# The end of a two-layer kernel reordered: the last eight skip terms go to TensorE, and the last norm's first four tiles are transposed together

## The reference

```
x      = silu(conv(proj))                       # 8 groups x 8 channel tiles of 128
y      = Y_diag + Y_off * decay + D * x         # D * x is the skip term
y      = y * rsqrt(mean(y*y) + eps) * norm_w * silu(gate)
h      = h + y @ out_proj.T                     # residual
n      = layernorm(h)
out    = h + n @ W_up.T + LoRA(chosen expert, n)
```

## Time and profile before

| | |
|---|---|
| median of 3 runs | 1755.25 us (1753.87 to 1755.78) |
| profiled execution, whole | 1755.16 us |
| its span in the trace | 1753.2 us |
| TensorE busy | 1686.0 us, 96% of the span |
| VectorE, ScalarE, GpSimd busy | 68%, 72%, 42% |
| mean granted TensorE clock | 0.98 |

### The profile page before, as it was taken

How to read it: one execution, slowest core, us unless ns; L and a number is a source line. 1 busy time by engine, 2 the same in 40 slices (tenths; PEclk the granted TensorE clock), 3 DMA queues, 4 the chain that set the end, 5 groups by cost and what they waited for, 6 DMA issues and landing times.

```text
span 1753.2 us, 26728 instructions
## 1 busy us (share of the span) xinstructions
PE 1686.0 (96%) x9420; PEld 1379.0 (79%) x9420; DVE 1192.9 (68%) x1868; ACT 1270.3 (72%) x2173; POOL 732.6 (42%) x794
## 2 busy tenths in 40 slices
PE   6998799999999999999999999999999999999978
PEld 5876577788888888888888888888888888888767
DVE  5665676866676767676766776677767676767773
ACT  3332138986888778877987798779877887888831
POOL 3543023444444344433444345344444444344550
PEclk9998799999999999999999999999999999999989
DMA  4310215323232323232333232323232323232401
GB/s 164 112 67 1 78 61 168 116 85 105 85 111 90 111 85 117 85 116 73 111 100 101 85 109 92 115 71 120 93 105 83 109 90 112 92 109 69 141 14 48
DMA packets 98564, 166.45 MB, mean 95 GB/s; under 512 B 11616, under 2 KB 49888, under 8 KB 96768
## 3 DMA queue, kind: packets, MB, share of 16 engines
q1 hardware_dynamic: 98432, 164.75, 28.9%
HBM read 158.43 MB, written 6.29 MB: 94 GB/s over the span
## 4 chain that ended last, share of the span: by engine, by line
PE 81%; DVE 4%; ACT 2%; issue 1%; POOL 0%; POOLq 0%; DVEq 0%; ACTq 0%
PE bank L203 22%; PE bank L205 21%; PE bank L204 21%; PE bank L1819 7%; PE bank L1829 4%; PE bank L1809 3%; PE bank L1887 1%; DVE m_xc L1556 1%; DVE m_gate L1556 0%; ACT m_mt L1318 0%; DVE m_xc L1490 0%; PE bank L1934 0%; DVE m_wo_l L1585 0%; DVE m_gate L1472 0%; PE bank L194 0%
## 5 line engine op out<-in xcount | busy, mean ns | idle before, releaser
L203 PE MATMUL bank<-xh,w_h 128*128 128x512 f32 x1152 | 463.4, 402 | 3.4 <-DVE m_xc L1556 2.9
L205 PE MATMUL bank<-xh,w_l 128*128 128x512 f32 x1152 | 451.5, 392 | 0.0
L204 PE MATMUL bank<-xl,w_h 128*128 128x512 f32 x1152 | 449.2, 390 | 0.0
L1233 POOL TENSOR_TENSOR m_z_l<-m_zg,m_z_h 128x512 fp32r<-128x512 f32 x128 | 177.4, 1386 | 572.7 <-ACT m_z_h L1394 572.7
L1318 ACT ACTIVATE m_mt<-m_mt,m_unit 128x128 f32<-128x128 f32 x1024 | 312.0, 389 | 0.0
L1212 POOL TENSOR_TENSOR w_l<-w_raw,w_h 128x512 fp32r<-128x512 f32 x144 | 187.2, 1300 | 231.1 <-ACT w_h L1285 231.1
L1567 DVE TENSOR_TENSOR x<-x,bank 128x512 f32<-128x512 f32 x128 | 87.8, 686 | 270.5 <-PE bank L205 270.2
L203 PEld LDWEIGHTS bank<-xh,w_h 128*128 128x128 f32 x1152 | 216.8, 188 | 55.6 <-issue 13.6
L205 PEld LDWEIGHTS bank<-xh,w_l 128*128 128x128 f32 x1152 | 216.5, 188 | 47.4
L1556 DVE SCALAR_TENSOR_TENSOR m_xc<-bank,m_par_conv,m_xc 128x1020 f32<-128x1020 f32 (+2 forms) x192 | 244.6, 1274 | 10.1 <-ACT m_xc L1297 5.2
L204 PEld LDWEIGHTS bank<-xl,w_h 128*128 128x128 f32 x1152 | 217.1, 188 | 41.3
(11 more groups left out here) (270 smaller groups left out, 2775.7 us busy)
## 6 DMA issues: line engine op xcount, KB each, us to landing
m_mt<-ncs_rows SPq DMA_DIRECT2D x128, 512.0 KB, 3.7
w_raw<-w_in SPq DMA_DIRECT2D x144, 256.0 KB, 3.1
m_wo_raw<-w_out_in SPq DMA_DIRECT2D x64, 256.0 KB, 5.1
m_e<-ecs_rows SPq DMA_DIRECT2D x128, 128.0 KB, 3.5
a_wo_raw<-wo_in SPq DMA_DIRECT2D x8, 1024.0 KB, 4.9
x<-x_in SPq DMA_DIRECT2D x8, 256.0 KB, 4.6
a_wq_raw<-wq_in SPq DMA_DIRECT2D x8, 256.0 KB, 4.5
x_saved<-x SPq DMA_DIRECT2D x1, 2048.0 KB, 8.5
```

Source lines behind the costliest of these rows:

```text
L203: nc.tensor.matmul(out, ah, bh, start=first, stop=False)
L204: nc.tensor.matmul(out, ah, bl, start=False, stop=False)
L205: return nc.tensor.matmul(out, al, bh, start=False, stop=last)
L1233: nc.gpsimd.tensor_tensor(z_l[:, s % 2, :, :], zg[:], f(z_h[:, s % 2, :, :]), ALU.subtract).then_inc(zl_ready, 1)
```

## The change

DVE no longer multiplies x by D in the last eight steps: four diagonal matrices are built once, and PE adds D * x into bank 4. `add_up` (in every group) issues the eight matmuls that need only z_h first and waits for z_l before the last four. Expert weight splits and the residual for tiles 0 and 1 move. The first four normalised tiles are transposed one after the other into banks 0, 1, 4, 5. The fourth `base` of each half moves behind `turn_lora`. The tiles xeh and xel lie elsewhere in memory, over first halves of two buffers that are used no more.

```diff
@@ turn_bank
-        return t % 2 if t < HT else (t + 1) % 2
+        return (0, 1, 4, 5)[t] if t < HT else (t + 1) % 2
@@ POOL, step / after run
-                if kind == "last" and NT + 2 <= s < NT + 6:
-                    (a_low if s < NT + 4 else base_low)((s - NT) % 2)
+                if kind == "last" and s in (NT + 2, NT + 3):
+                    a_low(s % 2)
                 if kind == "last" and s == STEPS - 2:
-                    for t in range(3):
-                        add_residual(t)
+                    add_residual(2)
+                    add_residual(3)
...
             run(step, prepare)
-            add_residual(3)
-            base_low(2)
-            base_low(3)
+            pool.wait_ge(xn_ready, HT)
+            for k in range(KT):
+                base_low(k)
@@ ACT, step
-                if kind == "last" and s in (NT + 2, NT + 3):
-                    ks = slice(2 * (s % 2), 2 * (s % 2) + 2)
-                    nc.scalar.activation(wb_h[:, ks, :], wb_raw[:, ks, :], ACT.Copy).then_inc(ew_hi, 1)
-                if kind == "last" and s == NT + 4:
-                    nc.scalar.activation(b_h, b_raw, ACT.Copy).then_inc(ew_hi, 1)
                 if kind == "last" and s == STEPS - 2:
                     act.wait_ge(crs_ready, 1)
-                    for t in range(HT):
+                    for t in (2, 3):
                         nc.scalar.activation(acc[:, t, :], ...).then_inc(scaled, 1)
+                    for ks in (slice(0, 2), slice(2, 4)):
+                        nc.scalar.activation(wb_h[:, ks, :], wb_raw[:, ks, :], ACT.Copy).then_inc(ew_hi, 1)
+                    nc.scalar.activation(b_h, b_raw, ACT.Copy).then_inc(ew_hi, 1)
@@ ACT, high / after run
             def high(t):
+                act.wait_ge(y_ready, at(LAST, STEPS - 1))
...
             high(0)
+            high(1)
+            high(2)
+            high(3)
             root_of_sums(1)
-            high(1)
             read_a(0)
-            high(2)
             read_a(1)
-            high(3)
@@ DVE, step
+                if s == NT - 1 and kind == "last":
+                    dve.wait_ge(w_split, tile_at(LAST, LEAD - 1))
+                    for ct in range(CT):
+                        nc.vector.tensor_scalar(d_mat[:, ct, :], ident[:], par_dn[:, CT + ct:CT + ct + 1], None,
+                                                ALU.mult).then_inc(d_ready, 1)
...
+                    whole = bank[:, 4, :].rearrange("p (c l) -> p c l", c=CT)
+                    by_tensor = kind == "last" and half == 1
+                    if by_tensor and s % 2 == 0:
+                        last = nc.vector.tensor_copy(y[:], whole)
-                    for ct in range(CT):
+                    for ct in range(0 if by_tensor else CT):
...
+                    if by_tensor and s % 2 == 1:
+                        dve.wait_ge(off_ready, pair(g, s))
+                        last = nc.vector.tensor_tensor(y[:], whole, off, ALU.add)
...
-                if kind == "last" and s == STEPS - 3:
+                if kind == "last" and s == STEPS - 2:
                     sums_to_scale(0)
+                    combine(0)
@@ DVE, low
-                dve.wait_ge(ew_lo, min(t + 1, 7))
@@ DVE, after run
+            add_out(LAST, STEPS - 2)
+            combine(1)
             statistics(0)
             statistics(1)
-            add_out(LAST, STEPS - 2)
             statistics(2)
...
             low(0)
+            low(1)
             variance_of_sums(1)
-            low(1)
+            low(2)
+            low(3)
             sums_to_scale(1)
             combine(4)
             combine(5)
-            low(2)
             combine(6)
-            low(3)
             combine(7)
@@ PE, diag
-                                            start=True, stop=True)
+                                            start=h < 2 or not (g == LAST and s >= NT),
+                                            stop=not (g == LAST and s >= NT))
+                if g == LAST and s >= NT:
+                    half, t = divmod(s, NT)
+                    pe.wait_ge(d_ready, CT)
+                    for ct in range(CT):
+                        last = nc.tensor.matmul(bank[:, 4, ct * P:(ct + 1) * P], d_mat[:, ct, :],
+                                                xc[:, half, ct, t * P:(t + 1) * P], start=False, stop=ct == CT - 1)
@@ PE, add_up
-                pe.wait_ge(zl_ready, at(g, s))
+                pe.wait_ge(zh_ready, at(g, s))
                 pe.wait_ge(acc_added, at(g, s - 1))
...
                 for ct in range(CT):
-                    last = three_pass(...)
+                    if t == 0:
+                        pe.wait_ge(wo_split, wo_at(g, half, ct))
+                    nc.tensor.matmul(bank[:, 7, :], z_h[:, s % 2, ct, :], wo_h[:, ct, :], start=ct == 0, stop=False)
+                    nc.tensor.matmul(bank[:, 7, :], z_h[:, s % 2, ct, :], wo_l[:, ct, :], start=False, stop=False)
+                pe.wait_ge(zl_ready, at(g, s))
+                for ct in range(CT):
+                    last = nc.tensor.matmul(bank[:, 7, :], z_l[:, s % 2, ct, :], wo_h[:, ct, :], start=False,
+                                            stop=ct == CT - 1)
@@ PE, after run
             sums(1)
-            turn_norm(0)
-            turn_norm(1)
-            products(0)
-            turn_norm(2)
-            products(1)
-            turn_norm(3)
-            products(2)
-            products(3)
             for t in range(HT):
-                base(t)
+                turn_norm(t)
+            for t in range(HT):
+                products(t)
+            base(0)
+            base(1)
+            base(2)
             turn_lora(0)
             turn_norm(4)
+            base(3)
...
-            for t in range(HT, NT):
-                base(t)
+            base(4)
+            base(5)
+            base(6)
             turn_lora(1)
+            base(7)
```

More of the change, by code:

```diff
@@ L836, in ssm_block @@
         gate = earlier.enter_context(nc.sbuf_tensor("m_gate", [P, 2, CT, TOKENS], F32))
+    sb("first_xc", [P, CT, TOKENS])
     xeh = sb("xeh", [P, NT, KT, P], F32R)
-    sb("second_xc", [P, CT, TOKENS])
+    sb("first_gate", [P, CT, TOKENS])
     xel = sb("xel", [P, NT, KT, P], F32R)
-    sb("second_gate", [P, CT, TOKENS])
     b_cm, c_cm = gate[:, 0, 2, :], gate[:, 0, 3, :]
@@ L877, in ssm_block @@
     csmall = small_part(6 * NT).rearrange("p (i t) -> p i t", i=6)
+    d_mat = small_part(CT * P).rearrange("p (c l) -> p c l", c=CT)
     dt_loaded = sem("dt_loaded")
@@ L960, in ssm_block @@
     combined = sem("combined")
+    residual_added = sem("residual_added")
     nvar_ready = sem("nvar_ready")
@@ L975, in ssm_block @@
     stored = sem("stored")
+    d_ready = sem("d_ready")
     TILES = PROJ_TILES
@@ L1269, in add_residual @@
                 pool.wait_ge(xs_loaded[0], 16)
-                pool.wait_ge(scaled, t + 1)
-                nc.gpsimd.tensor_tensor(acc[:, t, :], acc[:, t, :], xs[:, t, :], ALU.add).then_inc(combined, 1)
+                pool.wait_ge(scaled, t - 1)
+                nc.gpsimd.tensor_tensor(acc[:, t, :], acc[:, t, :], xs[:, t, :], ALU.add).then_inc(residual_added, 1)
             run(step, prepare)
-            add_residual(3)
-            base_low(2)
-            base_low(3)
+            pool.wait_ge(xn_ready, HT)
+            for k in range(KT):
+                base_low(k)
             pool.wait_ge(ew_hi, 4)
@@ L1644, in step @@
                             in1=bank[:, 4, ct * P:(ct + 1) * P], op0=ALU.mult, op1=ALU.add)
-                    if s % 2 == 1:
+                    if by_tensor and s % 2 == 1:
+                        dve.wait_ge(off_ready, pair(g, s))
+                        last = nc.vector.tensor_tensor(y[:], whole, off, ALU.add)
+                    elif s % 2 == 1:
                         last.then_inc(dx_added, 1)
@@ L1683, in statistics @@
             def statistics(t):
-                dve.wait_ge(combined, t + 1)
+                if t in (2, 3):
+                    dve.wait_ge(residual_added, t - 1)
+                else:
+                    dve.wait_ge(combined, t + 1 if t < 2 else t - 1)
                 return n.statistics(nc, t)
@@ L1714, in combine @@
             def combine(t):
-                dve.wait_ge(xs_loaded[1], 16)
+                dve.wait_ge(xs_loaded[t // HT], 16)
                 dve.wait_ge(acc_added, at(LAST, NT + t))
@@ L1833, in add_up @@
             def add_up(g, s):
-                pe.wait_ge(zl_ready, at(g, s))
+                pe.wait_ge(zh_ready, at(g, s))
                 pe.wait_ge(acc_added, at(g, s - 1))
                 half, t = divmod(s, NT)
-                if t == 0:
-                    pe.wait_ge(wo_split, wo_at(g, half, CT - 1))
                 for ct in range(CT):
-                    last = three_pass(nc, bank[:, 7, :], z_h[:, s % 2, ct, :], z_l[:, s % 2, ct, :],
-                                      wo_h[:, ct, :], wo_l[:, ct, :], ct == 0, ct == CT - 1)
+                    if t == 0:
```

(13 more changed lines are left out.)

## The result

The changed kernel takes 1740.26 us (median of four runs, 1737.69 to 1743.35) against 1755.5 for the kernel before: 0.9914 of its time (95% interval 0.9902 to 0.9926), 15.2 us less where 12.1 were forecast. Run again with the experiments it took 1738.63 (1737.87 to 1739.35), 0.9908 (0.9894 to 0.9921), 15.45 less than its neighbours. The profiled execution took 1737.69, with a span of 1735.9.

A forecast was written before the change was run, and what follows sets the result against it. The last eight steps were taken as bound by a chain round the engines, PE nearest to full. Savings of 9.4 + 0.2 + 2.5 = 12.1 us from 1755.16 gave 1743.1, range 1739 to 1748.

The forecast's parts named there:

- inner forecast: Whole kernel: a time of 1741 to 1745.5 us, given a chance of 0.40.
- Part 1: Last eight steps, D(8) to end of U(14): PE's waits go, PE bounds at full clock, 5.1 us less.
- Part 2: Last product U(15) and norm, up to the first transpose: 4.3 us less.
- part 3: First transpose to first base: 0.2 us less, two of four products at half clock.
- The price of the skip products: Steps 8 to 15: four added PE products cost 0.92 us per step, 7.4 in all.
- Rival C: Steps 8 to 15: the chain's waits stay and the products come on top, 1755.6 to 1762.9 us; chance 0.05.
- rival B: Last group: POOL contending with DVE, ACT's step 14 or y late, +1 to +3 us, 1745; chance 0.13.
- the old 5.1 us: Norm, last statistics to first transpose: 5.1 us before, some 1.5 from drawn-out small instructions; 2.9 forecast.
- The other way of rival A: Behind the norm and in the second half's products: no half clock, -2.3 and -1.3 us, 1739.5; chance 0.13.
- rival A: Clock behind the norm: all four products at half clock, one more base caught, +2.4 to +4 us; chance 0.22.
- Part 4: Both halves, turn_lora to lora: a base covers the waits for the LoRA operands, 2.5 us less.
- Rival D: Last eight steps: PE's waits only change names, half of the first saving lost, 1747 to 1749 us; chance 0.07.

The follow-up runs named there:

- splits early: Changed kernel with the expert weight splits back in steps 10 to 13 and POOL's last two behind the steps: 1744.02 us, 0.9936 of the kernel before.
- own banks: Changed kernel with the last group's U taking turns over banks 7, 0 and 6, and scale, combines, statistics, last add_outs and turn_norm(4) moved: 1735.76 us, ratio 0.9891.
- bases first: Changed kernel with the fourth base ahead of turn_lora in both halves: 1743.66 us, 0.9937 of the kernel before.
- old add_up: Changed kernel with add_up as before in every group, three passes per weight tile behind z_l and all four weight splits: 1741.61 us, ratio 0.9928.
- interleaved order: Changed kernel with the first four tiles' transposes between the products, in banks 0 and 1, and low and high as before: 1743.71 us, ratio 0.9935.

## Why the prediction was right, and where it was not

**Direction and size**: right. 1740.26 lies in the range of 1739 to 1748, 2.8 us below the number, for the reason given: PE's waits went and PE became the bound at full clock. It lies outside the inner forecast of 1741 to 1745.5, and that the sum is no further off is in part luck: parts 1 and 2 brought 0.9 less than forecast, part 3 and the second half's products 4.3 more.

**Which edit removes which wait** the prediction had too simple. It gave the z_l wait to the new order of U and the 4.1 us wait to the moved scale. With only the order back 1.6 us of wait for z_l return, and 6.4 when the skip is back on DVE as well. With only the scale back 1.5 us return for `add_out(12)`, and 3.1 when skip and order are undone too. The skip products, which relieve DVE as predicted, buy 1.6 us by themselves.

**The price of the skip products**: right. 0.92 was taken from A; 0.91 to 1.00 was measured. Rival C falls, since the chain's waits did not stay: D(8) to the end of U(14) shrank by 4.8 us with the products in it. (That doubled products cost their full time would be so under rival C too.)

**Part 1**: right within 0.3 (4.8 for 5.1). What I had not seen late is `add_out(13)`: it stands behind `sums_to_scale(0)`, whose five instructions of four columns take 3.1 us here. I had allowed for their drawing out with z_h(15) alone. DVE in order of time in the changed kernel:

```profile
1671.92 0.16 DVE L127 RECIPROCAL w_raw<-w_raw 128x4 f32<-128x4 f32 x1
1672.12 0.80 DVE L128 TENSOR_TENSOR w_raw<-w_raw 128x4 f32<-128x4 f32 x1
1672.95 1.20 DVE L129 TENSOR_TENSOR w_raw<-w_raw 128x4 f32<-128x4 f32 x1
1674.18 0.66 DVE L130 TENSOR_SCALAR w_raw<-w_raw 128x4 f32<-128x4 f32 x1
1674.87 0.16 DVE L131 TENSOR_TENSOR w_raw<-w_raw 128x4 f32<-128x4 f32 x1
```

U(14) waits 0.47 for it: rival B at a small scale. The 0.87 ahead of U(15) was in the forecast, with 0.7.

**Part 2**: 3.7 for 4.3. Most of the 0.6 is `combine(1)`: 0.7 forecast, and it took 1.56 beside z_l and the squares on POOL. The account of the old 5.1 us held: with POOL away from the norm L128 takes 0.16, with POOL back (splits early) 0.68 and its neighbours 1.19. But I counted the moved splits with no more than these 1.5; taken back alone they cost 4.9, of which 3.0 stand ahead of the first transpose. In their new place they fall beside `low` and `sums_to_scale(1)`, where L129 and L130 take 1.23 and 1.20. POOL is done at 1694.68, before `combine(4)` begins at 1695.12, so the combines are not drawn out as the prediction feared (2.74 us for four). It also called all these instructions ones with two SBUF inputs, which L127 and L130 are not. The cover held, for PE has no wait there in the changed kernel.

**Part 3 is the term that was mis-sized**: 0.2 forecast, 3.0 measured. I took two of the four products at 1.2 GHz (2.73 each). The half-clock stretch was shorter, some 3 us, and it fell whole on the sixteen transposes, which lose little by it: 3.1 us to the first product at half clock, 2.1 (own banks) without, since normalisation sets the pace. All four products ran at 1.43 in the mean, 5.74 in all. Part of this is luck: in bases first, with the same code up to here, the half clock reached into product(0), which took 2.70, and in old add_up it took 2.37. The other way of rival A named this end at -2.3, and -1.3 in the products of the second half, where 1.5 was measured, though its condition, no half clock at all, was not met behind the norm. Both together are 4.3 more than the sum held. The interleaved order shows the counterpart: product(0) takes 2.73 us at 0.50, and the stretch is 4.1 longer, 2.0 of it a wait.

**Part 4**: right, 2.4 for 2.5. With the fourth base ahead the waits return as 0.95 and 1.39; the edit costs more than 2.5, since the clock falls behind it. The 1.5 us gained in products 4 to 7 were not in the sum, and the cover does not secure them: in five kernels that have it they are lost again.

**Rival D** (waits only change names) fell: 1.3 us are left of the 11.0 of the earlier trace rows.

**What adds up, and what stays open.** The single undoings of the skip, add_up, the bases, the order of the turns and the splits sum to 18.7, more than the 15.45 of the whole. Three of them (add_up, bases, splits) contain the half clock around product(4), 4.6 us together, and the kernel before pays for it once, 1.5. Counted once the sum is 15.6; with differences that are uncertain by about two microseconds each, so close an agreement may be chance. Left open are what makes the clock fall around product(4) in some kernels, what differs in the first 47 us between executions of the same code, and what the execution of 1743.35 us lost, of which there is no trace.

## What to carry to other kernels

Read a wait's price with what the clock does behind it, and put into that stretch the work that another engine paces anyway (here transposes behind a normalisation), not the dense products. Keep a chain of tiny VectorE instructions clear of GpSimd's wide ones: move the GpSimd work, even where both engines have room. When a relieved engine starts to wait for an accumulator to be read out, give the accumulator a second bank before judging what the relief was worth: with it, and what was moved along with it, these products' worth rose from 1.6 to 4.7 us. And where executions of the same code are up to 2.7 us apart before the changed place is reached, read small effects from a mark just ahead of it.

## What the runs showed of the hardware

The drawing out of VectorE is not in proportion to the data: a 128x4 instruction of 0.16 us takes 0.66 to 1.23 beside a 128x512 subtraction on GpSimd, as if it waited for a part of that to pass, or for the whole (one such subtraction takes 1.26). So does L130, which has a single tensor operand. The Trainium skill (GPSIMD Engine Reference, section 8, Key points) names VectorE instructions in a 2-port perf mode or with two SBUF inputs. L128 and L129 are of the second kind, and the trace agrees; whether L130 ran in a mode of the first kind, no trace here tells. Not every VectorE instruction is drawn out: `low` (L1728), with one operand in PSUM, takes 0.69 beside the same subtractions.

Behind the norm of the changed kernel it is VectorE alone that gives way: the four base splits, 1404 ns each in the earlier trace rows, take 1.26 each in a row. Elsewhere GpSimd gives way as well. In the kernel before, a split of the same shape that began 0.3 us behind VectorE's 128x1024 product took 2.26:

```profile
1688.42 5.04 POOL L1269 TENSOR_TENSOR xl<-m_gate,xh 128x512 fp32r<-128x512 f32 x4 [4.80 <-DVE m_wo_raw L1723]
```

```profile
1663.82 2.26 POOL L1262 TENSOR_TENSOR xl<-m_gate,xh 128x512 fp32r<-128x512 f32 x1
```
